# Graph convolution on Trainium2: a third gathered chunk a turn is built on other engines, SyncE bringing 96 of its 128 rows

## What is computed

```python
filters = silu(edge_attr @ fW1 + fb1) @ fW2 + fb2
messages = (x[src] @ dW + db) * filters
aggregated = segment_sum(messages, dst, num_segments=n)
out = x + silu(aggregated @ uW1 + ub1) @ uW2 + ub2
```

## Time and profile before

| | us |
|---|---|
| median of 3 runs | 3998.57 (3992.8 to 4001.38) |
| the profiled execution, its time | 3996.17 |
| its span | 3994.3 |
| convolution, first to last gather | 2092.7 to 3979.6 |

### The profile page before, as it was taken

One profiled execution on the slowest core, in us unless ns is written; L12 is line 12 of the kernel. 1 busy time (PEld: TensorE's weight loads), 2 busy tenths in 40 slices (PEclk: granted clock), 3 DMA queues, 4 the chain that ended last, 5 costly groups with the idle time before them and its releaser, 6 DMA issues. The chain is left out here.

```text
span 3994.3 us, 88540 instructions
## 1 busy us (share of the span) xinstructions
PE 3385.6 (85%) x14177; PEld 2645.2 (66%) x14178; DVE 2914.9 (73%) x9541; ACT 2120.9 (53%) x10279; POOL 2970.5 (74%) x3130
## 2 busy tenths in 40 slices
PE   4788888888888888888868999899899899988988
PEld 2566666666666666666656777677677677777766
DVE  7888888888888888888865666566666566665664
ACT  5455555555555555555533555555555555555552
POOL 6777777777777777777757777777777777777776
PEclk7555555555555555555556666766867767677676
DMA  4222222222222222222225333323333333333332
GB/s 126 58 62 62 62 63 62 62 62 64 62 62 62 64 62 63 62 64 61 63 51 143 80 81 80 83 76 81 83 78 80 81 79 82 78 82 81 79 81 62
DMA packets 194037, 292.21 MB, mean 73 GB/s; under 512 B 85234, under 2 KB 137517, under 8 KB 188842
## 3 DMA queue, kind: packets, MB, share of 16 engines
q0 software_dynamic: 99136, 206.49, 21.9%
q1 hardware_dynamic: 89500, 40.45, 4.1%
q10 hardware_dynamic: 4840, 40.55, 3.4%
HBM read 268.69 MB, written 15.70 MB: 71 GB/s over the span
## 5 line engine op out<-in xcount | busy, mean ns | idle before, releaser
L63 POOL DMA_INDIRECT ae_xg<-table,ae_idx x1592 | 1502.3, 944 | 491.3 <-issue 487.7
L63 POOL DMA_INDIRECT ce_xg<-table,ce_idx x1506 | 1429.0, 949 | 465.6 <-issue 454.0
L1473 ACT COPY ce_held<-sums 128x1 f32 x6880 | 751.9, 191 | 329.3 <-issue 325.2
L1003 PE MATMUL ae_ps_k<-ae_xg,ae_e 128*96 128x129 f32 x3224 | 881.4, 432 | 0.0
L1003 PEld LDWEIGHTS ae_ps_k<-ae_xg,ae_e 128*96 128x96 f32 x3224 | 688.6, 276 | 126.4 <-issue 117.0
L1508 PEld LDWEIGHTS ce_ring<-ce_fw,ce_hid 128*128 128x128 f32 x3228 | 594.9, 281 | 156.3 <-issue 90.8
L1508 PE MATMUL ce_ring<-ce_fw,ce_hid 128*128 128x128 f32 x3228 | 642.9, 376 | 50.0 <-DVE ce_msg L1633 49.9
L1598 DVE COPY ce_held<-sums 128x1 f32 x4128 | 507.5, 153 | 118.7 <-issue 117.8
L1539 PE MATMUL ce_ps_h<-ce_ea,ce_fw 50*128 50x384 f32 x1076 | 561.5, 655 | 34.0 <-DMA ce_ea<-in_edge_attr 19.1
L915 ACT ACTIVATE ae_upper<-ring 128x576 f32<-128x576 f32 x269 | 175.2, 651 | 670.5 <-DVE ring L1180 670.5
L1456 ACT ACTIVATE ce_hid<-ce_ps_h,ce_fb 128x768 f32<-128x768 f32 x269 | 242.2, 900 | 513.7 <-issue 381.6
(11 more groups left out here) (192 smaller groups left out, 3760.1 us busy)
## 6 DMA issues: line engine op xcount, KB each, us to landing
ae_stage<-table SPq DMA_DIRECT2D x2560, 0.5 KB
ce_stage<-table SPq DMA_DIRECT2D x2560, 0.5 KB
ce_ea<-in_edge_attr ACTq DMA_DIRECT2D x88, 450.0 KB
ae_xg<-table,ae_idx POOLq DMA_INDIRECT x1592
ce_xg<-table,ce_idx POOLq DMA_INDIRECT x1506
sums<-in_x SPq DMA_DIRECT2D x7, 448.0 KB, 4.9
sums<-features SPq DMA_DIRECT2D x1, 3136.0 KB
table<-sums SPq DMA_DIRECT2D x6, 462.0 KB, 3.8
```

Of the source, the lines that this page charges most:

```text
L63: eng.indirect_dma_start(out=out, out_offset=None, in_=table[:, :], in_offset=bass.IndirectOffsetOnAxis(ap=idx, axis=0)).then_inc(done, 16)
L1003: last = nc.tensor.matmul(ps_k[0:KEYS, 0:D + 1], by_chunk[s % 3][:, c, :], xg[:, s % XS, c, 0:D + 1], start=(c == 0), stop=(c == count - 1))
L1473: last = nc.scalar.copy(held[:, m, k:k + 1], by_node[:, bass.ds(node, 1)])
```

## The change

In the convolution alone:
- **POOL.** The last chunk of slots 1, 3 and 4 is left out of the gathers in every turn from 2 to 44 (`gather_units_beside`). That makes 36 + 36 gathers in turns 0 and 1, 33 in each of turns 2 to 43 and 27 in turn 44 (whose slot 4 is gathered with five chunks instead of four, the fifth unused): 1485.
- **SP.** `load_beside` takes the place of `load_indices`. In each turn 1 to 42 it copies 96 rows (48 in each half turn) for the next turn's slot 4, partitions 32 to 127, and delivers them in the next turn with one DMA after the index load and the output store of v = 0. Register loads stay at 16 addresses for 16 DMAs.
- **The other 32 rows** of that chunk are columns (a third `Column`, 14 by DVE and 18 by ACT). The shares are now 160 a turn on ACT (as before) and 128 on DVE (96 before). PE has a third product a turn, of 32 rows.
- **Copies.** A column is copied as four bytes (`u8`, 128x4) at a byte offset that stands ready in the register, instead of one fp32 at a column number. The offsets are made once at the start: DVE scales the list (`drawn`), and SP, after waiting for that, copies it into `columns`.
- **Loops.** ACT's and DVE's loops (`hinted_finishing_turns`, `column_turns`) are built with `hint_back_edge=True`; DVE's is now one loop over turns 2 to 43. PE's, POOL's and SP's have no hint.

```diff
+def hinted_finishing_turns(nc, engine, body):
...
+    with nc.Fori(OPEN + 1, SHUT, engines=[engine], hint_back_edge=True) as i:
+        body(i, False, SL)
...
-COLUMNS = (Column((0, 1, 2), 5, 1), Column((3, 4, 5), 2, 3))
+CARRY_SLOT = 4
+COLUMNS = (Column(1, 5, False, 58, 70), Column(3, 1, True, 56, 72), Column(CARRY_SLOT, 3, True, 14, 18))
-HALF = 48
-PIECE = 16
+ROWS = 96
+ROW_TURNS = TURNS - 3
...
+SCALAR = Share([32, 32, 16] * 2, [range(c.vector, c.count) for c in COLUMNS])
+VECTOR = Share([24, 24, 16] * 2, [range(c.vector) for c in COLUMNS])
...
+def gather_units_beside(pool, passes, table, xg, idx, idx_in, gathered, xg_free, pool_turn):
...
+            for s in range(count):
+                if s % LOAD == 0:
+                    pool.wait_ge(idx_in[s // LOAD], 16 * (r * TURNS + i + 1))
+                pool.wait_ge(xg_free, r * UNITS + (XS if first else i * SL + s + 1))
+                pool.sem_inc(pool_turn, 1)
+                for c in range(CH - 1 if s in TO and takes(i) else chunks_of(i, s)):
...
+    def collect(self, nc, sp, i, v, b):
+
+        size, share = 4 * D, ROWS // LOADS
+        for first in range(v * share, (v + 1) * share, READ):
+            starts = nc.values_load_multi_w_load_instructions(
+                self.lists[:, bass.ds((i - 1) * ROWS + first, READ)], engines=[mybir.EngineType.SP], min_val=0, max_val=(N - 1) * size,
+                skip_runtime_bounds_check_because="a source is a node")[1]
+            for p, start in enumerate(starts, P - ROWS + first):
+                sp.dma_start(self.stage[p:p + 1, b, :].bitcast(u8), self.bytes[:, bass.ds(start, size)]).then_inc(self.rows_in, 16)
...
+    def deliver(r, i, b):
+
+        sp.wait_ge(rows.rows_in, 16 * ROWS * (r * ROW_TURNS + i - 1))
+        sp.sem_inc(rows.turn, 1)
+        sp.wait_ge(xg_free, r * UNITS + i * SL + CARRY_SLOT + 1)
+        sp.dma_start(xg[P - ROWS:P, CARRY_SLOT, CH - 1, :], rows.stage[P - ROWS:P, b, :]).then_inc(rows.carried, 16)
+
+    def turn(r, i, b, collect=True, bring=True):
+
+        for v in range(LOADS):
+            read(r, i, v)
+            sp.dma_start(idx[v][:, :],
+                         a["src"][bass.ds((i + 1) * LOADS + v, 1), :, 0:P // 2, :].rearrange("u o p c -> (u o) p c")).then_inc(idx_in[v], 16)
+            ahead(r, i + 1, v)
+            if v == 0:
+                beside(r, i)
+                if bring:
+                    deliver(r, i, 1 - b)
+                if isinstance(i, int) and i == 0:
+                    listed(r)
+            if collect:
+                rows.collect(nc, sp, i, v, b)
+            if v == 0 and bring:
+                sp.wait_ge(rows.carried, 16 * (r * ROW_TURNS + i - 1))
+                sp.sem_inc(rows.turn, 1)
...
+            sp.dma_start(drawn[:, :], a["column_rows"][:, :]).then_inc(lists_in, 16)
+
+            sp.wait_ge(scaled, 2)
+            for k, share in enumerate((SCALAR, VECTOR)):
+                sp.dma_start(columns[32 * k:32 * k + 1, 0:COLUMN_TURNS * share.total].rearrange("o (t c) -> o t c", c=share.total), by_row[k]).then_inc(table_in, 16)
...
-                    for k, node in enumerate(sources_at(nc, mybir.EngineType.DVE, columns, i, m, e0, e1), e0):
-                        last = nc.vector.tensor_copy(held[:, m, k:k + 1], by_node[:, bass.ds(node, 1)])
+                    starts = sources_at(nc, mybir.EngineType.DVE, columns[32:33, :], (i - 1) * VECTOR.total + VECTOR.start(s), VECTOR.counts[s])
+                    for (m, k), start in zip(VECTOR.slot(s), starts):
...
+                        one = nc.vector.tensor_copy(held_bytes[:, 4 * (m * P + k):4 * (m * P + k) + 4], by_byte[:, bass.ds(start, 4)])
...
+            nc.vector.tensor_scalar(drawn[:, :], drawn[:, :], 4.0, 2.0 * 4 * NW, ALU.mult, ALU.add).then_inc(scaled, 1)
```

More of the change, by code:

```diff
@@ L495, in start_pass, with sources_at @@
     dve.sem_inc(begun, 1)
[L498 to L502, removed]
+def sources_at(nc, engine, row, first, count):
+    for k in range(0, count, READ):
+        yield from nc.values_load_multi_w_load_instructions(row[:, bass.ds(first + k, min(READ, count - k))], engines=[engine],
+                                                            min_val=2 * 4 * NW, max_val=2 * 4 * NW + 4 * (N - 1),
                                                             skip_runtime_bounds_check_because="a source is a node")[1]
@@ L528, in finishing_turns @@
     body(SHUT, False, REST)
+def hinted_finishing_turns(nc, engine, body):
+    body(0, True, SL)
+    for i in range(1, OPEN + 1):
+        body(i, False, SL)
+    with nc.Fori(OPEN + 1, SHUT, engines=[engine], hint_back_edge=True) as i:
+        body(i, False, SL)
+    body(SHUT, False, REST)
 def opens(i):
@@ L575, in places, with takes, column_rows, moved_rows @@
     return not (isinstance(i, int) and not first <= i < first + COLUMN_TURNS)
-def column_chunks():
+def takes(i):
+    return not (isinstance(i, int) and i < 2)
+def column_rows(rows):
     turn = np.arange(2, TURNS)
-    return np.concatenate([(turn * SL + to) * CH + CH - 1 for to in TO])
+    chunk = [rows[(turn * SL + to) * CH + CH - 1] for to in TO]
+    return np.concatenate([chunk[m][:, e:e + 1] for share in (SCALAR, VECTOR) for m, e in share.held], 1)
+def moved_rows(rows):
+    return rows[(np.arange(2, 2 + ROW_TURNS) * SL + CARRY_SLOT) * CH + CH - 1, P - ROWS:].reshape(1, -1)
 def column_at(r, i, m):
@@ L602, in chunks_of, with landed_by @@
     return REST_CH if isinstance(i, int) and i == TURNS - 1 and s == REST - 1 else CH
[L605 to L609, removed]
+def landed_by(pace, r, i, s, carried=0, j=0):
     if s != CARRY_SLOT:
@@ new lines, in load_beside, with read @@
+def load_beside(nc, sp, a, h, idx, idx_in, gathered, landed, rows, xg, xg_free, ahead, beside, listed):
+    def read(r, i, v, count=SL):
+        s = min(v * LOAD + LOAD, count) - 1
+        sp.wait_ge(gathered[s], landed_beside(r, i, s))
+    def deliver(r, i, b):
[20 more added lines that the diff above has]
+                sp.sem_inc(rows.turn, 1)
+    passes = pass_count(sp, h)
+    with sp.Fori(0, passes) as r:
+        for v in range(LOADS):
+            ahead(r, 0, v)
+        turn(r, 0, 1, False, False)
+        turn(r, 1, 0, True, False)
+        turn(r, 2, 1)
+        with sp.Fori(1, ROW_TURNS // 2) as p:
+            turn(r, 2 * p + 1, 0)
+            turn(r, 2 * p + 2, 1)
+        turn(r, TURNS - 2, 0, False)
+        for v in range(LOADS):
+            read(r, TURNS - 1, v, REST)
+            sp.dma_start(idx[v][:, :], a["src"][v, :, 0:P // 2, :]).then_inc(idx_in[v], 16)
+        beside(r, TURNS - 1)
+    for v in range(LOADS):
+        sp.wait_ge(idx_in[v], 16 * (passes * TURNS + 1))
+    sp.sem_inc(landed, 1)
@@ L1461, in collect @@
                 def collect(i, s):
[L1463 to L1467, removed]
-                        act.sem_inc(begun, 1)
[L1469 to L1476, removed]
+                    if s == 0:
+                        act.wait_ge(table_in, 16 * (r + 3))
+                        act.sem_inc(begun, 1)
+                    starts = sources_at(nc, mybir.EngineType.Activation, columns[0:1, :], (i - 1) * SCALAR.total + SCALAR.start(s), SCALAR.counts[s])
+                    for (m, k), start in zip(SCALAR.slot(s), starts):
+                        if k == SCALAR.first[m]:
+                            act.wait_ge(s_column, column_at(r, i, m) + 1)
+                            act.sem_inc(begun, 1)
+                        one = nc.scalar.copy(held_bytes[:, 4 * (m * P + k):4 * (m * P + k) + 4], by_byte[:, bass.ds(start, 4)])
+                        if k == SCALAR.last[m]:
+                            one.then_inc(s_other, 1)
+                hinted_finishing_turns(nc, mybir.EngineType.Activation, turn)
             for k, (a0, a1) in enumerate(HALVES):
```

120 lines of the change are left out of this document (77 added, 43 removed).

## The result

| | before | changed |
|---|---|---|
| median | 3999.73 us | 4236.57 us (4222.0 to 4262.25, 4 runs) |
| the profiled execution, its span | 3994.3 | 4237.7 (its time 4239.52) |
| gathers | 1506 | 1485 |
| SP's turn, mean of turns 2 to 42 | paced by POOL, 41.7 | 47.96 |

The ratio is **1.0603** (95%: 1.0549 to 1.0656): slower, as forecast, but by 237 us instead of 134; the time lies outside the range of 4065 to 4200.

The account below looks back on a forecast made before the run. SP's queue was taken to set the pace in place of POOL: 2214.8 us, then 41 turns at 45.5 to 4080.3, plus 35.8, 13.8 and 1.9, giving 4131.8; 2.4 more for the median gives 4134 us, range 4065 to 4200.

Parts of the forecast that it names:

- SP's turn: SP's queue, one turn: 31.7 us of work, 13.6 for 32 more rows, 0.5 for delivery, landing wait; taken as 45.5 us.
- What bounds it: Convolution: SP's queue sets the pace in place of POOL, its 10.0 us of slack a turn being spent; chance 0.76.
- The gathers, 21 fewer: POOL: 1506 - 1485 gathers at 1.251 us each, 26.3 us to gain; POOL's own turn becomes 41.3 us.
- gather length, DVE, ACT and the start: Gathers stay at 0.95 us; DVE costed at nothing, ACT hidden; the start hidden, 0 to 5 us if not.
- the sum for the profiled execution: Whole span: SP's load at 2170.3, 44.5, 41 turns at 45.5, then 35.8, 13.8 and 1.9 us, giving 4131.8.
- the reading from one turn: SP's turn from one timeline turn: halves of 16.4 and 14.2 us, plus 13.6 for the added rows, makes 44.2 us.
- a wait that is already met costs less than what is counted beside it: SP's turn: the reason given for taking 45.5 us, nearer the middle of the readings 44.2 and 45.8.
- the sum of the parts, 45.8: SP's turn: 31.7 us of work, 13.6 for two more batches of 16 rows and 0.5 for delivery every turn.
- Landing of rows: SP's wait for the 96 rows, which come about 2 us after the last issue: 0 to 1.5 us a turn.
- The end: After SP's last load: about 2 us to land, 33.8 for 27 gathers, 13.8 from last gather to span's end.
- Rival 3: DVE's 128 byte copies a turn hold POOL's gathers: 4252 us at 51 ns a copy, 4815 at the whole; chance 0.11.
- Its upper bound, 47.3 us a turn: SP's turn at 45.8 us plus the full 1.5 us landing wait, giving 4134 + 74 = 4208 us.

Follow-up runs that it names:

- the fast kernel: The changed kernel with 64 rows a turn by SP, 64 columns of that chunk (30 by DVE, 34 by ACT) and even shares, nothing left out: 3968.90 us, ratio 0.9937.
- the first run: The changed kernel with hint_back_edge also on SP's loop over turns 3 to 42: 4164.97 us, ratio 1.0419.

## Why the forecast was right and wrong

- **What bounds it: right.** SP's queue sets the pace; the earlier trace rows left 10.0 us a turn for 14.1. SP's load in turn 2 came at 2214.25, forecast 2214.8. The gathers, 21 fewer, are worth 26 us once SP is out of the way (the run with 32 rows left out, and the fast kernel), and gather length, DVE, ACT and the start cost nothing, as costed. The gain is below SP's loss in the changed kernel, not absent.
- **The term that failed: SP's turn**, "45.5 us", measured 47.96. It missed 2.46 x 41 = 101 us of the 108 by which the sum for the profiled execution was off (4239.5 against 4131.8); 7 more came at the end. Three measured parts make up the turn: 44.7 us of work (the run with later delivery; the reading from one turn was 44.2), 2.2 us of loop end and about 1.3 of waiting for rows. The work was well sized. What failed is that SP's loop end had no term at all, and that the step "a wait that is already met costs less than what is counted beside it" put the turn 0.3 us under the sum of the parts, 45.8, before any landing.
- **Loop ends, the missing term.** The prediction named the loop-end gaps of ACT and DVE, and did not look for SP's. They were there before: eight branches in 2250 to 3750 us with 34.8 us of standstill, once in four turns. These 1.0 us a turn sat unseen in the 31.7 us taken for SP's work, so the 45.8 held less than half of what loop ends then cost; 45.8 - 1.0 is the 44.7 of work. The change makes the ends twice as frequent and takes the slack that covered them. They are 88 us in all; the first run alone got 72 of them back.
- **Landing of rows, the mis-sized one.** I allowed "0 to 1.5 us a turn" and, at 45.5 against the two readings' middle of 45.0, took about 0.5. It is 52.0 us in 16 waits, 1.3 a turn, at the upper end; the run with later delivery shows it avoidable.
- **The end.** From SP's last load of v = 0 (4180.76) to the span's end are 56.9 us, not the 49.6 of the sum. POOL's timeline has the gap:

```profile
4181.71 0.94 POOL L63 DMA_INDIRECT ce_xg<-table,ce_idx  x1 [0.30 <-issue]
4189.42 0.94 POOL L63 DMA_INDIRECT ce_xg<-table,ce_idx  x1 [6.76 <-DMA ce_idx<-in_src]
```

  The index load took 7 us to land where I had 2. From the packets of the trace, 39 of the changed kernel's 84 index loads from 2208 us on were issued within 6 us behind ACT's load of edge attributes (450 KB), and their last packet ended 4.9 us after the end of the issue in the median, against 1.5 us for the other 45; in the kernel before none of 86 was issued so, and the median was 1.7. That would also explain the waits for rows. The two go together in the trace; no run separated them, so this stays open.
- **Rival 3, the byte copies holding gathers: refuted.** 947 ns a gather beside 128 of them a turn, and the fast kernel with words is not faster. The Trainium skill's rule ("SBUF — State Buffer", "Who interferes with whom") does not show here for copies of four bytes in a partition; the gather of 4.25 us stood beside a far larger fill. The Trainium skill ("VectorE: DVE Perf Modes", "What auto-detection actually checks") lets two sides of equal size meet its condition too, so the evenness of four bytes does not clearly set them apart from word copies, as the prediction had it; those left a gather at 946 ns as well.
- **Range.** Its upper bound, 47.3 us a turn, held only the loop ends hidden in the 31.7 us and no late landing at the end, and the range then cut the sum's 4208 to 4200. With 48.0 us a turn and 7 us for the last landing the same sum gives 4134 + 103 + 5 = 4242, against 4237 measured.

## What to carry to other kernels

Before moving work to an engine that "has slack", add up its whole queue for one period: issues, register loads, waits for what it issued itself, and loop ends. Slack hides all of them at once, and they all come back when it is spent; of 32 moved rows, 13.6 us a turn met 10 us of slack, and 3.5 us more appeared. Of the amounts that were run, the best was the one that leaves slack (64 rows), not the most that seems to fit; nothing between 64 and 96 was tried. And a helper's parameters can carry a hidden condition: shares that looked free cost from 160 us (4186 against 4027 expected) to 580 (4551 against 3969) because of where a list was read.

## What the runs showed of the hardware

- **A load of 16 registers from SBUF took 1.0 us on ACT and 1.1 on DVE when it began at a multiple of 4 numbers (16 bytes) of the list, and 3.4 and 3.6 us, up to 3.9, when it began anywhere else.** Of 8 numbers, 0.55 and 1.8 us on ACT; of 3 numbers, some 0.75 us on DVE from any place. The places are counted from the list's start, in the three kernels whose shares or stride mix them. 316 us came from one number of padding a turn (4024.79 against 4340.77).
- **A loop end without a hint held SP for 4.4 us on average (88.2 / 20), ACT for 3.8 in the kernel before (155.7 / 41) and DVE for up to 4.3.** With the hint SP and DVE stood still for under 0.25 us in every run. ACT did so in eight runs, but in the fast kernel and its variant with word copies it stood still for 4.3 and 4.2 us on average in spite of the hint; why is open, since the kernel with 64 rows and uneven shares has as long a loop on ACT (417 recorded instructions a turn against 411) and no such gap. A shorter SP loop (64 rows) had no such gap without a hint. The Trainium skill ("Runtime: NRT & Kernel Launch", "Instruction fetch mechanics") says that a taken branch whose target isn't in the window of two pages must fetch it first; SP's long loop against its short one agrees with that, and no run here measures the window.
- **Copies:** a word copy with a computed address repeats every 101 ns on ACT, a byte copy with a ready one every 95; on DVE 126 and 106 (medians). Size and address changed together, so what either is worth alone is not shown; the four bytes cost no more than the word.
